# Weights and context loaded with swapped axes, and expert splits placed in cross-attention's buffers

## The reference

```
x = x + self_attention(layernorm(x), w_qkv, w_out)        # 16 heads of 32, causal mask
q, k_new, v_new = n @ wq.T, n @ wk.T, n @ wv.T            # n = layernorm(x), per batch
k = concat(ctx, k_new); v = concat(ctx, v_new)            # 256 + 256 keys
x = x + softmax(q @ k.T / sqrt(512)) @ v @ wo.T           # cross-attention, one head of 512
probs = softmax(n @ wg); e = argmax(probs)                # n = layernorm(x), 8 experts
x = x + probs[e] * (n @ W[e].T + b[e])                    # one expert for each token
```

## Time and profile before

| | us |
|---|---|
| median of 3 runs | 864.57 |
| lowest, highest | 862.69, 866.25 |
| the profiled execution | 868.03 |
| its span, first to last instruction | 866.3 |
| PE busy in the span | 762.7 |
| DVE, ACT, POOL busy | 529.1, 370.4, 312.2 |

### The profile page before, as it was taken

The page is one execution under the profiler, slowest core; times in us unless marked ns, Lnnn a source line. Parts: engine busy times, 40 slices in busy tenths (PEclk is TensorE's granted clock), DMA queues, the critical chain, the costliest instruction groups (busy, mean ns, idle before and its releaser), DMA issues. The chain is left out here.

```text
span 866.3 us, 19948 instructions
## 1 busy us (share of the span) xinstructions
PE 762.7 (88%) x6424; PEld 688.1 (79%) x6425; DVE 529.1 (61%) x1557; ACT 370.4 (43%) x1145; POOL 312.2 (36%) x456
## 2 busy tenths in 40 slices
PE   4798989898989999757999999999999985739995
PEld 4787979888888888646899998989899974637884
DVE  4678685868686867546565655556464533834664
ACT  4476675757575767534423232313133220622221
POOL 3376574757565656641000101010101101124662
PEclk9999999999999999879999999999999997868998
DMA  9643343444444434306712425060502111765630
GB/s 345 147 114 94 105 101 106 93 118 93 116 93 118 93 94 115 101 1 208 286 52 72 99 23 113 8 121 20 101 30 67 59 15 49 168 163 152 199 122 24
DMA packets 49575, 90.90 MB, mean 105 GB/s; under 512 B 11390, under 2 KB 11518, under 8 KB 49408
## 3 DMA queue, kind: packets, MB, share of 16 engines
q1 hardware_dynamic: 43872, 77.80, 34.2%
q0 software_dynamic: 5664, 12.61, 4.7%
HBM read 51.95 MB, written 18.77 MB: 82 GB/s over the span
## 5 line engine op out<-in xcount | busy, mean ns | idle before, releaser
L398 ACT ACTIVATE prob<-prob,nmax 128x128 f32<-128x128 f32 (+1 forms) x256 | 114.5, 448 | 77.9 <-DVE nmax L576 77.9
L337 POOL TENSOR_TENSOR pt_part<-pt_rest,pt_part 128x384 bf16<-128x384 f32 x128 | 117.8, 921 | 10.2
L335 POOL CAST pt_part<-pt_rest 128x384 bf16<-128x384 f32 x128 | 67.4, 527 | 113.5 <-DVE pt_rest L585 112.1
L576 DVE CUSTOM_DVE_ANT_0 prob<-a_s,mask 128x128 f32<-128x128 f32 (+1 forms) x256 | 80.2, 350 | 4.1 <-PE a_s L457 3.2
L585 DVE TENSOR_TENSOR pt_rest<-a_t,pt_part 128x384 f32<-128x384 f32 x128 | 70.8, 553 | 7.2 <-ACT pt_part L408 7.0
L408 ACT CAST pt_part<-a_t 128x384 bf16<-128x384 f32 x128 | 60.6, 473 | 32.3 <-PE a_t L470 32.1
L470 PE MATMUL a_t<-ident,prob 128*128 128x128 f32 x384 | 63.5, 275 | 12.2 <-DVE pt_rest L585 11.8
L457 PE MATMUL a_s<-stack 96*128 96x256 f32 x256 | 61.8, 324 | 0.2 <-DVE nmax L576 0.2
L470 PEld LDWEIGHTS a_t<-ident,prob 128*128 128x128 f32 x384 | 45.2, 141 | 17.9 <-issue 15.3
L488 PE MATMUL a_o<-pt_part,v_part 128*32 128x256 bf16 (+1 forms) x1536 | 40.4, 258 | 14.2 <-POOL pt_part L337 13.9
L922 ACT CAST b_kt_hi<-b_bank 128x256 fp32r<-128x256 f32 (+1 forms) x48 | 20.5, 445 | 66.1 <-PE b_bank L56 65.2
(11 more groups left out here) (217 smaller groups left out, 1986.1 us busy)
## 6 DMA issues: line engine op xcount, KB each, us to landing
stack<-qk SPq DMA_DIRECT2D x192, 128.0 KB, 2.4
stage<-in_w SPq DMA_DIRECT2D x8, 1024.0 KB, 8.9
xin<-in_x SPq DMA_DIRECT2D x8, 512.0 KB, 3.6
xr<-in_x SPq DMA_DIRECT2D x8, 512.0 KB, 3.6
x<-xr SPq DMA_DIRECT2D x8, 512.0 KB, 2.8
xin<-x SPq DMA_DIRECT2D x8, 512.0 KB, 8.9
b_cin<-in_ctx SPq DMA_DIRECT2D x8, 512.0 KB, 3.5
xr<-x SPq DMA_DIRECT2D x8, 512.0 KB
```

Of the source, the lines that this page charges most:

```text
L335: nc.gpsimd.tensor_copy(pt_part[1][:, t % NPT, :], rest).then_inc(pt_mid_done, 1)
L337: nc.gpsimd.tensor_tensor(pt_part[2][:, t % NPT, :], rest, pt_part[1][:, t % NPT, :], ALU.subtract).then_inc(pt_done, 1)
L398: a = nc.scalar.activation(prob[:, e % NPROB, cols], prob[:, e % NPROB, cols], ACT.Exp, scale=-1.0, bias=nmax[:, e, q:q + 1], accum_out=rs ...
L576: m = nc.vector.tensor_tensor_reduce(out=prob[:, s % NPROB, cols], in0=s_ps[s % 2][:, q, 0:P * (q + 1)], in1=mask[:, P * (1 - q):], scale= ...
```

## The change

The host now hands over the four matrices, W and a second copy of the context with their last two axes swapped. So no weight and no context is transposed on the chip; the instructions split what the DMA brought to SBUF. The high and low parts of all eight experts (`ExpertWeights`) are allocated before cross-attention, and cross-attention's own split matrices lie in parts of these places (`PLACES`), so that an expert's split can be written as soon as its place has been read for the last time, during batch 7.

The jobs w and C are gone. ScalarE and VectorE split wq and wk in four pieces each, and POOL splits wv and wo and makes its constants only then. The context's keys are split by ScalarE and VectorE behind s1. Experts are cast by ScalarE before and behind batch 7's jobs and subtracted by VectorE (0, 3, 7) and POOL (1, 2, 4, 5, 6). The count of tokens stands behind o3 instead of o1. The banks of the ring are numbered from 0 in every batch.

```diff
+class ExpertWeights:
...
+    def load(self, sp, w, e):
+        wait(sp, self.split[e % STAGED], e // STAGED)
+        sp.dma_start(self.stage[e % STAGED][:], w[e].rearrange("(c p) n -> p c n", p=P))\
+            .then_inc(self.loaded[e % STAGED], 16)
+
+    def high(self, nc, act, e):
+        act.wait_ge(self.loaded[e % STAGED], 16 * (e // STAGED + 1))
+        nc.scalar.copy(self.place(e)[0], self.stage[e % STAGED][:]).then_inc(self.hi_done, 1)
+
+    def low(self, engine, e):
+        hi, lo = self.place(e)
+        engine.wait_ge(self.hi_done, e + 1)
+        engine.tensor_tensor(lo, self.stage[e % STAGED][:], hi.bitcast(F32), ALU.subtract)\
+            .then_inc(self.split[e % STAGED], 1)
...
+        PLACES = {"q": 0, "k": 1, "v": 2, "o": 6}
+        wt_hi, wt_lo = ({n: experts.place(e)[part] for n, e in PLACES.items()} for part in range(2))
+        kt_hi, kt_lo = experts.place(3)
+        xt_hi, xt_lo = experts.place(4, 0, S)
+        qt_hi, qt_lo = experts.place(4, S, D)
+        v_hi, v_lo = experts.place(5)
+        pt_hi, pt_lo = experts.place(7, 0, S)
+        ot_hi, ot_lo = experts.place(7, S, D)
...
-        ORDER = ("X0 X1 s0 s1 C0 C1 q0 q1 p0 p1 q2 q3 o0 o1 o2 o3 k0 y0 y1 k1 k2 k3 v0 Y0 Y1 v1 l0 l1").split()
-        FRONT = "XCqkv"
+        ORDER = ("X0 X1 s0 s1 q0 q1 p0 p1 q2 q3 o0 o1 o2 o3 k0 y0 y1 k1 k2 k3 v0 Y0 Y1 v1 l0 l1").split()
+        FRONT = "Xqkv"
         LAST = [j for j in ORDER if j[0] not in FRONT]
-        PROLOGUE = ("wq0 wq1 wq2 wq3 wk0 wk1 X0 X1 wk2 wk3 q0 q1 C0 C1 q2 q3 wv0 wv1 k0 k1 wv2 wv3 k2 k3 wo0 v0 wo1 v1 "
-                    "wo2 wo3").split()
+        PROLOGUE = "X0 X1 q0 q1 q2 q3 k0 k1 k2 k3 v0 v1".split()
...
             sp.dma_start(raw[2][:], chunks(wv)).then_inc(w_in[2], 16)
+            load_ctx_t(0)
             sp.dma_start(raw[3], chunks(wo)).then_inc(w_in[3], 16)
+            sp.dma_start(cin[:], batch_rows(ctx, 0)).then_inc(c_in, 16)
             sp.wait_ge(x1_out, 16 * (B - 1))
             sp.wait_ge(x1_last_out, 16)
             sp.dma_start(xr[:], batch_rows(x1, 0)).then_inc(xr_in, 16)
             sp.dma_start(wg_sb[:], chunks(wg)).then_inc(wg_in, 16)
             sp.wait_ge(xn_ready, TB)
             sp.dma_start(xin[:], batch_rows(x1, 1)).then_inc(x_in, 16)
+            for i, done, count_of in ((0, w_split, DC), (1, w_split, 2 * DC), (2, wv_split, 2)):
+                sp.wait_ge(done, count_of)
+                experts.load(sp, w, i)
+            sp.wait_ge(ct_split, 1)
+            load_ctx_t(1)
             sp.wait_ge(c_split, 1)
-            sp.wait_ge(job_done, done_at("C1", -1))
             sp.dma_start(cin[:], batch_rows(ctx, 1)).then_inc(c_in, 16)
 
-            for i, n in enumerate("qkv"):
-                sp.wait_ge(job_done, done_at(f"w{n}3", -1))
-                sp.dma_start(stage[i][:], w[i].rearrange("(c p) h -> p c h", p=P)).then_inc(expert_in[i], 16)
-
-            sp.wait_ge(job_done, done_at("wo3", -1))
+            sp.wait_ge(wo_split, 2)
...
             def batch(n, more, load):
 
                 if load:
+                    sp.wait_ge(ct_split, n + 2)
+                    load_ctx_t(n + 2)
                     sp.wait_ge(xn_ready, (n + 2) * TB)
                     sp.dma_start(xin[:], batch_rows(x1, n + 2)).then_inc(x_in, 16)
                     sp.wait_ge(c_split, n + 2)
-                    sp.wait_ge(job_done, done_at("C1", n))
                     sp.dma_start(cin[:], batch_rows(ctx, n + 2)).then_inc(c_in, 16)
+                if not more:
+                    for e in range(STAGED, E - 1):
+                        experts.load(sp, w, e)
...
+            experts.load(sp, w, E - 1)
...
+            for i, name, done in ((2, "v", wv_split), (3, "o", wo_split)):
+                pool.wait_ge(w_in[i], 16)
+                nc.gpsimd.tensor_copy(wt_hi[name], raw[i][:] if i < 3 else raw[i]).then_inc(done, 1)
+                pool.wait_ge(done, 1)
+                nc.gpsimd.tensor_tensor(wt_lo[name], raw[i][:] if i < 3 else raw[i], wt_hi[name].bitcast(F32),
+                                        ALU.subtract).then_inc(done, 1)
+                if name == "v":
+                    rstd_ln2(1)
             routing.constants(nc, pool)
-            rstd_ln2(1)
             rstd_ln2(2)
             rstd_ln3(0)
...
             rstd_ln3(B - 2)
-            routing.store_entries(nc, pool, tick_pool, B - 3, True)
-            routing.store_entries(nc, pool, tick_pool, B - 2, True)
+            routing.store_entries(nc, pool, tick_pool, B - 3)
+            routing.next_tokens(nc, pool, tick_pool, B - 3)
+            for e in (1, 2):
+                experts.low(nc.gpsimd, e)
+            routing.store_entries(nc, pool, tick_pool, B - 2)
+            experts.low(nc.gpsimd, 4)
             rstd_ln3(B - 1)
+            routing.next_tokens(nc, pool, tick_pool, B - 2)
+            for e in (5, 6):
+                experts.low(nc.gpsimd, e)
 
         @block.scalar
         def _(act):
...
+            act.wait_ge(job_done, done_at("v1", B - 2))
+            for e in range(STAGED):
+                experts.high(nc, act, e)
             batch(B - 1)
+            for e in (3, 4, 5):
+                experts.high(nc, act, e)
+            act.wait_ge(job_done, done_at("y1", B - 1))
+            for e in (6, 7):
+                experts.high(nc, act, e)
 
...
             pe.wait_ge(wg_in, 16)
+            pe.wait_ge(wo_split, 2)
             pe.wait_ge(routing.consts, Routing.CONSTS)
...
                     job(j, n)
-                    if j == "o1" and has_routing(n):
+                    if j == ("o3" if order(n) is ORDER else "o1") and has_routing(n):
                         routing.count(nc, pe, n - 1)
...
+                    if j == "s1" and order(n) is ORDER:
+                        ctx_t_lo(n + 1)
                     if j == "o3" and order(n) is ORDER:
                         ctx_lo(n + 1)
+                    if j == "o3" and order(n) is LAST:
+                        experts.low(nc.vector, 3)
...
-            for i in range(DC):
-                w_job(i)
             routing.count(nc, pe, B - 1)
-            for i in range(DC, W_JOBS):
-                w_job(i)
             pe.wait_ge(owner_done, 1)
-            pe.wait_ge(w_split, W_JOBS)
+            experts.all_split(pe)
...
-            for i in range(EARLY, W_JOBS):
-                w_lo_part(i)
+            experts.low(nc.vector, 7)
...
+    columns = lambda t: np.swapaxes(np.asarray(t), -1, -2)
+    arrays = {"x": rows(x), "ctx": rows(ctx_2048), "ctx_t": columns(ctx_2048).reshape(B * D, S), "w_qkv": L0_attn_w_qkv,
+              "w_out": L0_attn_w_out, "wq": columns(L0_xattn_wq), "wk": columns(L0_xattn_wk),
+              "wv": columns(L0_xattn_wv), "wo": columns(L0_xattn_wo), "wg": L0_ffn_wg, "w": columns(L0_ffn_W),
```

More of the change, by code:

```diff
@@ new lines, with __init__, place, all_split @@
+class ExpertWeights:
+    ON_POOL = (1, 2, 4, 5, 6)
+    def __init__(self, nc, cx, stage, loaded):
+        sb = lambda n: cx.enter_context(nc.sbuf_tensor(n, [P, DC, E * D], F32R))
+        sem = lambda n: cx.enter_context(nc.semaphore("e_" + n))
+        self.hi, self.lo, self.stage, self.loaded = sb("w_hi"), sb("w_lo"), stage, loaded
+        self.hi_done = sem("hi_done")
+        self.split = [sem(f"split{i}") for i in range(STAGED)]
+    def place(self, e, start=0, stop=D):
+        return [t[:, :, e * D + start:e * D + stop] for t in (self.hi, self.lo)]
+    def load(self, sp, w, e):
[10 more added lines that the diff above has]
+            .then_inc(self.split[e % STAGED], 1)
+    def all_split(self, engine):
+        for i in range(STAGED):
+            engine.wait_ge(self.split[i], len(range(i, E, STAGED)))
@@ L745, in cross_attention @@
+def cross_attention(nc, ident, routing, x1, x1_out, x1_last_out, x1_first_in, ctx, ctx_t, wv, wo, wg,
+                    x2n, x2n_out, xin, xr, x2_sb, xn3_sb, bias, bias_sb, bias_in, stage, stage_in, w, experts):
     scale = float(D) ** -0.5
@@ L812, in route_after, with jobs_in, w_piece @@
             return "q3" if order(n) is ORDER else "p1"
+        def jobs_in(n):
+            return PROLOGUE if isinstance(n, int) and n < 0 else order(n)
         def bank(j, n):
[L815 to L818 removed]
+            return ring[jobs_in(n).index(j) % RING]
+        def w_piece(w, i):
+            return w[:, :, i * P:(i + 1) * P]
         def parts_of(j, n):
@@ L955, in wait_bank @@
             def wait_bank(j, n):
-                if isinstance(n, int) and n < 0:
-                    before, of = PROLOGUE.index(j) - RING, -1
-                    if before < 0:
-                        return
-                    last = PROLOGUE[before]
-                else:
-                    before = order(n).index(j) - RING
-                    if before >= 0:
-                        last, of = order(n)[before], n
-                    elif isinstance(n, int) and n == 0:
-                        last, of = PROLOGUE[before], -1
-                    else:
```

(25 more changed lines are left out.)

158 lines of the change are left out of this document (75 added, 83 removed).

## The result

Nine timed runs of each kernel: before, median 864.16 us (860.07 to 866.25); changed, 859.24 us. One of the nine ran with a lowered clock throughout (921.07 us) and is left out of what follows; the other eight lie between 855.47 and 860.16. The ratio is 0.9938, 95% interval 0.9915 to 0.9961: faster by 0.6%, 5.4 us, where 11.5 were forecast. The sign was right and the time lies in the range, but above the forecast's own 847 to 858.

The account below looks back on a forecast made before the run. TensorE's work bounds the batches, waiting the time afterwards. Tail -14.7, transposes -5.5, rows +6.5, prologue +2.2 sum to -11.5 us: 856.5 profiled, 853 timed; forecast 847 to 858 (chance 0.52), range 841 to 862.

Parts of the forecast that it names:

- Prologue: Before batch 0: POOL's late constants and held-up VectorE splits start it 0.5 us later; with 1.7 cold start, 2.2 lost.
- Batches: Cross-attention batches: 5.5 us saved without context transposes, 6.5 lost because x1's rows arrive late.
- the transposes: Batches: dropping the context's eight transposes saves 0.79 us in each of 7 batches, 5.5 in all.
- the rows: Batches: x1's rows, queued behind the context's load, land in 4.3 us; TensorE stalls 1.3 in batches 1 to 5; 6.5 lost.
- Tail: Last batch to first expert product: no expert transposes; barrier 3.9 us later, product 25.0 after it; 14.7 saved, bounds 9 to 18.
- rival C: End of cross-attention: POOL's last subtractions slip behind a held-up indirect write or late entries; 4 to 8 lost, 857 to 861; chance 0.15.
- The step from the trace to the time: Whole kernel: profiled time forecast at 856.5 us, less 3.5 because before's timed median lay that far below its profiled execution: 853.1.
- A: Prologue, batches and tail: neither engine held up and x1's rows arrive in time; 839.4 us; chance 0.22.
- B: Batches: x1's rows land 8.9 us after issue or later, 34.1 lost instead of 6.5; 880.7 in all; chance 0.07.
- D: Tail: the last expert loads arrive so late that expert work still ends the wait; chance 0.04 together with the rest.

Follow-up runs that it names:

- rows_first: Changed kernel with SyncE loading the rows of x1 before the wait for the context's split and the context's load; median 852.17 us, ratio to before 0.9844.
- best: Changed kernel with x1's rows loaded first, subtractions of experts 5, 6 and casts of 6, 7 behind the barrier, POOL's constants before its splits; 839.27 us, ratio to before 0.9711.
- wo_dve: Changed kernel with wo subtracted by VectorE instead of POOL, TensorE waiting for it only before batch 0's y0; median 851.88 us, ratio to before 0.9854.
- late_lows: Changed kernel with the subtractions of experts 5 and 6 moved from POOL to VectorE behind the block tables; median 857.07 us, ratio to before 0.9897.
- best2: On top of best: wo cast by ScalarE and subtracted by VectorE, expert 4 subtracted by VectorE instead of POOL; median 838.27 us, ratio to before 0.9661.

## Why the prediction was right in kind and wrong in size

The step that failed is the tail's term: 14.7 us saved were forecast, 10.0 are measured. Means of three traces each, in the prediction's own terms:

- **Prologue, forecast +0.5 (and 1.7 of cold start behind it).** Measured 30.48 to 29.97, -0.5, and 2.5 of cold start (rows_first against best, 270.10 to 267.56, with a granted clock of 0.99 and 1.00). Right, down to the mechanism: constants at 424.5, splits held up beside POOL. What was missed is the pair L1159: the prediction looked only for VectorE instructions with two SBUF inputs, and these have one large input. The Trainium skill (SBUF — State Buffer, section "Who interferes with whom") also says that a VectorE `tensor_scalar` in a 2-port mode takes the pair of ports that GpSimd uses for a whole instruction; the traces agree that the pair stands (6.18, 2.19 and 0.99, by what POOL does), though no row says in which mode it runs, and I had left that half of the rule out. It cost nothing here, since POOL's constants came later still.
- **Batches, forecast -5.5 for the transposes and +6.5 for the rows.** The transposes were worth 7.4 (275.00 to 267.55 in best, no stops in either), the rows cost 7.95. The two errors cancel, and that is luck. The first error has two parts, which together make the 1.07 between the periods 39.32 and 38.25. The transposes of the context cost 0.88 a batch and not 0.79, because the first group of products behind them also takes 0.56 until the next one starts, where 0.48 is usual. And in the jobs y and v, 12 groups of four matmuls in a batch, all but the first group behind another kind of job now start every 0.91 instead of every 0.93. That is 0.2 a batch, and a term the prediction did not have. The second error: from the transposes of p to y0 TensorE needs 12.53 (513.45 to 525.98) where rows_first needs 11.15 (515.76 to 526.91), so the stall is 1.4 in this batch and not 1.3. The two pauses of 0.33 and 0.72 show only 1.05 of it. Groups of 0.64 otherwise start every 0.48, and each stop loses this overlap of 0.16 as well. Over five batches that makes most of the 7.95, and one batch took 0.6 more than the others. The landing behind the context's load was 4.2, near the 4.3 of the sum; the landings of 5.3 and more, which the prediction read as a sign of the queue's order, were of rows issued ahead of the context's load, so they did not bear on it.
- **Tail, forecast -14.7; the term that failed.** In the traces it is 80.5 to 70.5, -10.0. Of the 4.7 missing, 3.0 are on the changed kernel's side. The barrier, forecast 42.5 after s0, comes at 44.7: POOL goes on from the entries' landing about 1.2 later than I put it (33.5 after s0 against 32.35), with the indirect write held up for 2.0 beside VectorE's split of expert 3, which is the mechanism of rival C; and 1.49 pass between POOL's last work and the barrier, which I had not counted (0.28 behind VectorE's copy in before, whose place POOL took). That the held-up write is the whole cause of the 1.2 is argued, not shown: no run moved that split alone, and with the same hold-up wo_dve had the landing at 32.1. Behind the barrier it is 25.9 instead of 25.0. The other 1.7 are on the side of before: its 82.25 came from one execution in which two transfers were slow (11.82 and 8.41). The change removes the second of these waits, the eighth expert's, and the first is 8.1 to 9.0 in the changed kernel.
- **The step from the trace to the time.** "Its like would be 856.5 ... 3.5 lower, so I predict 853.1." The profiled execution was above its median, and I took that surplus off the changed kernel as well. That is only right if the surplus lies in parts that both kernels have. Part of it lay in the stretch behind the barrier (43.60, 2.5 above the mean of the three), whose waits for expert weights go; the changed kernel's profiled executions (858.14, 861.47, 859.21) lie around its own median, not above it.

Together the traces give -7.8 in the mean of three (spans 865.5 and 857.8): prologue -0.5, batches +3.05 with the cold start (+2.7 forecast), tail -10.0, and -0.3 for self-attention and the rest. The timed medians give -4.9 and, in the second measurement, -5.5; by the ratios it is -5.4 and -6.7. Self-attention alone ends between 390.4 and 397.7 in thirteen traces of the same instructions, and TensorE's granted clock in that stretch goes with it: 0.98 in the shortest (late_lows), 0.97 in the two near 393.6, 0.96 between 395.0 and 396.3, 0.95 in the two above. Three traces don't settle 2 us against that, and the rest stays open.

Of the rivals, A (nothing held up) fell with the first trace; B did not happen, with landings of 4.2; C came partly true through its first half. Its 857 to 861 holds the result, but partly by luck: it gave 4 to 8 for a late barrier, and the barrier is 2.1 late; the rest of the missing 4.7 has the other causes above. D did not happen, since expert loads are no longer in the chain.

## What to carry to other kernels

When a change removes a wait, price the wait from several executions; one trace's slow transfer is not yours to save. When work goes to POOL, look at every VectorE instruction beside it that works from SBUF to SBUF, short ones too, and at what stands behind them. When a load gets a wait in front of it in a queue, every load behind inherits that wait: here one swapped pair of lines was worth 8 us, more than the whole change gained.

## What the hardware showed that was not expected

- A VectorE instruction on 2 elements per partition took 2.03 us instead of 0.17 beside a POOL subtraction (0.17 with POOL quiet, best2). The subtraction L674 on 128x16 from SBUF took 2.40 instead of 0.17 in batch 7; it ended at 715.00, POOL's of expert 2 at 714.96. The subtraction from PSUM beside POOL's of wv kept its 0.42.
- POOL's indirect write took 3.03 and 2.45 instead of about 1.0 each time VectorE subtracted two SBUF tensors beside it, and ended 0.8 to 0.9 after VectorE did.
- Groups of four 512-column matmuls in y and v start every 0.91 us in the changed kernel and every 0.93 in the kernel before, at a granted clock of 1.00 in both. All their operands lie in other places, and the PSUM banks are numbered anew; which of this counts was not tried. Two groups of the kernel before and then two of rows_first, both in y0:

```profile
524.72 1.09 PE L56 MATMUL b_bank<-b_wot_lo,b_ot_hi 128*128 128x512 f32 x4
525.65 1.09 PE L56 MATMUL b_bank<-b_wot_hi,b_ot_lo 128*128 128x512 f32 x4
...
527.84 1.07 PE L56 MATMUL b_bank<-w_lo,w_hi 128*128 128x512 f32 x4
528.75 1.07 PE L56 MATMUL b_bank<-w_hi,w_lo 128*128 128x512 f32 x4
```
